# Three query groups of each batch with weights stationary in the second product of a two-batch attention block

## The reference, cut to what matters

```
qkv  = x @ w_attn + b_attn                  # x: (2, 4096, 256), float32
attn = softmax(q @ k.T / 16 + causal mask)  # per batch, 4096 x 4096
x    = layernorm(x + (attn @ v) @ w_proj + b_proj)
scores = x @ w_router;  top = the 3072 highest of 4096 per batch
x    = layernorm(x + (gelu(x @ w_block) for rows in top, x for the others))
```

## Time and profile before

| | |
|---|---|
| time, median of 3 runs | 978.8 us (977.38 to 978.82) |
| the profiled execution's own time | 978.79 us, of which the span is 977.1 us |
| TensorE (PE) busy | 942.2 us, 96% of the span, 4940 matmuls |
| weight loads (PEld) busy | 800.5 us, 82%, beside the matmuls |
| VectorE busy | 768.5 us, 79% |
| ScalarE busy | 638.7 us, 65% |
| GpSimd busy | 281.1 us, 29% |

### The profile page before, as it was taken

One profiled execution on the slowest core, in us unless ns is written; L12 is line 12 of the kernel. 1 busy time (PEld: TensorE's weight loads), 2 busy tenths in 40 slices (PEclk: granted clock), 3 DMA queues, 4 the chain that ended last, 5 costly groups with the idle time before them and its releaser, 6 DMA issues.

```text
span 977.1 us, 15396 instructions
## 1 busy us (share of the span) xinstructions
PE 942.2 (96%) x4940; PEld 800.5 (82%) x4940; DVE 768.5 (79%) x1472; ACT 638.7 (65%) x1006; POOL 281.1 (29%) x436
## 2 busy tenths in 40 slices
PE   8899999999999999999999999999999999998991
PEld 6788888888888888888888888888788888887770
DVE  5789697966876695688688979797898789549877
ACT  3466576764864595478466757567698668438893
POOL 5422214324041033514232231422403303201162
PEclk9999999999999999999999999999999999999996
DMA  6543343443343345567632433434678634427835
GB/s 203 195 136 108 98 152 119 129 136 102 108 151 109 97 130 162 159 197 239 208 120 85 159 119 98 141 108 156 200 248 280 195 97 124 143 79 251 305 102 173
DMA packets 89378, 149.52 MB, mean 153 GB/s; under 512 B 7761, under 2 KB 25810, under 8 KB 89298
## 3 DMA queue, kind: packets, MB, share of 16 engines
q1 hardware_dynamic: 89298, 148.54, 47.8%
HBM read 108.66 MB, written 39.85 MB: 152 GB/s over the span
## 4 chain that ended last, share of the span: by engine, by line
PE 87%; DVE 6%; issue 2%; ACT 2%; POOL 1%; DVEq 0%; ACTq 0%; POOLq 0%
PE sbank L507 36%; PE fbank L507 12%; PE obank L1022 11%; PE obank L1020 11%; PE obank L1021 11%; PE fbank L1101 1%; PE fbank L1294 1%; DVE ring_lo L986 1%; PE mbank L936 1%; DVE tail L1706 1%; DVE ring L967 1%; PE mbank L957 1%; DVE runmax L898 1%; ACT ring L974 1%; ACT parts L981 0%
## 5 line engine op out<-in xcount | busy, mean ns | idle before, releaser
L507 PE MATMUL sbank<-qT,xT 128*128 128x512 f32 (+2 forms) x1728 | 409.8, 377 | 1.5 <-issue 1.5
L507 PEld LDWEIGHTS sbank<-qT,xT 128*128 128x128 f32 x1728 | 305.7, 188 | 55.2 <-issue 2.2
L861 ACT COPY ring<-sbank 128x512 f32<-128x512 f32 (+3 forms) x288 | 157.4, 549 | 173.8 <-PE sbank L507 116.5
L1020 PE MATMUL obank<-ring_lo,vs 128*128 128x512 f32 (+3 forms) x576 | 218.8, 380 | 5.1 <-issue 1.7
L1022 PE MATMUL obank<-parts,vs 128*128 128x512 f32 (+3 forms) x576 | 216.1, 375 | 0.0
L1021 PE MATMUL obank<-parts,vs 128*128 128x512 f32 (+3 forms) x576 | 215.8, 375 | 0.0
L986 DVE TENSOR_TENSOR ring_lo<-ring,parts 128x1024 fp32r<-128x1024 f32 (+4 forms) x176 | 178.6, 1025 | 26.5 <-ACT parts L981 25.5
L903 DVE TENSOR_TENSOR runmax<-ring,runmax 128x1024 f32<-128x1024 f32 x84 | 106.1, 1264 | 89.0 <-ACT ring L861 88.2
L981 ACT CAST parts<-ring 128x1024 fp32r<-128x1024 f32 (+4 forms) x176 | 145.5, 834 | 46.8 <-PE obank L1022 46.5
L967 DVE TENSOR_TENSOR ring<-ring,mbank 128x1024 f32<-128x1024 f32 (+4 forms) x176 | 159.6, 949 | 8.4 <-PE mbank L957 8.4
L974 ACT ACTIVATE ring<-ring 128x1024 f32<-128x1024 f32 (+4 forms) x176 | 144.0, 845 | 16.9 <-DVE ring L967 16.7
(11 more groups left out here) (214 smaller groups left out, 1004.8 us busy)
## 6 DMA issues: line engine op xcount, KB each, us to landing
vs<-v_scratch SPq DMA_DIRECT2D x288, 256.0 KB, 2.8
v_scratch<-vnew SPq DMA_DIRECT2D x30, 512.0 KB, 3.1
xres<-x SPq DMA_DIRECT2D x16, 512.0 KB, 4.5
out<-tail SPq DMA_DIRECT2D x32, 256.0 KB, 3.3
x_scratch<-xres SPq DMA_DIRECT2D x14, 512.0 KB, 3.0
y_scratch<-yb SPq DMA_DIRECT2D x14, 512.0 KB, 4.3
tail<-x_scratch SPq DMA_DIRECT2D x28, 256.0 KB, 3.1
tail<-y_scratch SPq DMA_DIRECT2D x28, 256.0 KB, 3.9
```

The source lines that it names most:

```text
L507: mm = eng.matmul(o, lhs(lh, k), rhs(rh, k), start=n == 0, stop=n == len(todo) - 1)
L861: act.copy(slot(n)[:, c0:], sbank[n % NSS][:, c0:]).then_inc(a_copy, 1)
L1020: pe.matmul(o, vh, lo_, start=i == 0, stop=False)
```

## The change

The constant `STRAIGHT` = 3 marks the groups g = 0, 1 and 2 of each batch (G = 0, 1, 2, 8, 9, 10). For these:

- in `values` the scores become the stationary factor (128 keys by 128 queries) and the values stream (256 channels). A tile makes three matmuls of 256 columns for each block of 128 queries that it meets, into `obank[t // 2]`, so the outputs stand there with queries on the partitions. Each bank then takes two query blocks; only the first matmul into a bank has the start flag;
- there is no copy to `ot_sb`, no transpose and no `("o", G, j)` fill; `evac` reads `obank` itself once the group's last tile is done;
- the next group's first tile of `values` waits for `v_h`, that is, for the four additions of `evac`, and no longer for `a_ot`.

The counts of `a_ot` are taken over the other ten groups (`turned`). The tables of the planner, `PREFER_US` and `MARGIN_US`, get other numbers as well.

```diff
+STRAIGHT = 3
 PREFER_US = {"ffn flo": 100, "final load": 100, "project xlo": 100, "last chain": 60, "last router": 60,
-             "row_max reduce": 60, "project qhi": 60, "attention_out residual": 60, "project qlo": 60,
-             "attention_out stats": 60, "ffn fhi": 60, "scores copy": 30, "softmax hi": 30, "final scale": 30,
-             "row_max": 8, "scores hide": 8, "prepare xlo": 8, "project xhi": 8, "project vhi": 8,
-             "project vlo": 4, "softmax lo": 4, "ffn gelu": 4, "softmax exp": -4, "softmax z": -4,
-             "final result": -4, "ffn aggr": -8, "attention_out router": -8, "late": -8, "attention_out aggr": -8,
-             "final pick": -15, "attention_out score": -30}
+             "project qhi": 60, "attention_out residual": 60, "project qlo": 60, "attention_out stats": 60,
+             "ffn fhi": 60, "attention_out score": 60, "scores copy": 30, "softmax hi": 30, "final pick": 15,
+             "row_max": 8, "scores hide": 8, "prepare xlo": 8, "project vhi": 8, "row_max reduce": 4,
+             "project xhi": 4, "project vlo": 4, "softmax lo": 4, "ffn gelu": 4, "project load": 4,
+             "attention_out evac": 4, "softmax exp": -4, "softmax z": -4, "final result": -4, "ffn aggr": -8,
+             "attention_out router": -8, "late": -8, "attention_out aggr": -8, "attention_out istd": -8,
+             "final scale": -15, "final choose": -30, "prepare": -30}
...
-             "out": 1.5, "scores hide": 1, "values load": 0.6, "ffn aggr": 0.6, "final_roots": 0.6,
-             "row_max reduce": 0.3, "project load": 0.3, "proj": 0.3, "ffn stats": 0.3, "last": 0.3,
-             "attention_out stats": 0.3}
+             "out": 1.5, "scores hide": 1, "ffn store": 1, "values load": 0.6, "ffn aggr": 0.6,
+             "final_roots": 0.6, "row_max reduce": 0.6, "project load": 0.3, "proj": 0.3, "ffn stats": 0.3,
+             "last": 0.3, "attention_out stats": 0.3}
...
+    straight = lambda G: groups[G][1] < STRAIGHT
+    turned = lambda G: sum(not straight(H) for H in range(G))
...
-        out_fills += [("o", G, 0), ("o", G, 1)] + (block_fills(G) if G < LATE else [])
+        out_fills += ([] if straight(G) else [("o", G, 0), ("o", G, 1)]) + (block_fills(G) if G < LATE else [])
...
                 if i == 0:
-                    if G:
-                        pe.wait_ge(a_ot, CC * G)
+                    if G and straight(G - 1):
+                        pe.wait_ge(v_h, QT * G)
+                    elif G:
+                        pe.wait_ge(a_ot, CC * turned(G))
...
-                for c in range(CC):
+                for t in range(i or 0, QT) if straight(G) else ():
+                    o = obank[t // 2][:, t % 2 * C:(t % 2 + 1) * C]
+                    own = slice(t * P - c0, (t + 1) * P - c0)
+                    vh, vl = (vs[:, n % NV, h, :] for h in range(2))
+
+                    pe.matmul(o, lo_[:, own], vh, start=i == 0 and t % 2 == 0, stop=False)
+                    pe.matmul(o, hi_[:, own], vh, start=False, stop=False)
+                    mm = pe.matmul(o, hi_[:, own], vl, start=False, stop=t % 2 == 1 and (last or g == 0 and i == t))
+                for c in () if straight(G) else range(CC):
...
-            at("act", "attention_out ot", lambda act: ot(act, 0))
-            if G < len(groups) - 1:
+            if not straight(G):
+                at("act", "attention_out ot", lambda act: ot(act, 0))
+            if not straight(G) and G < len(groups) - 1:
                 at("act", "attention_out ot", lambda act: ot(act, 1))
...
-            o_halves = lambda j: bank_of(("o", G, j))[:, :].rearrange("p (t c) -> p t c", t=2)
+            o_bank = lambda j: obank[j] if straight(G) else bank_of(("o", G, j))
+            o_halves = lambda j: o_bank(j)[:, :].rearrange("p (t c) -> p t c", t=2)
...
             def evac(dve, j):
-                filled(dve, ("o", G, j))
+                if straight(G):
+                    dve.wait_ge(p_pv, first_tile[G + 1])
+                else:
+                    filled(dve, ("o", G, j))
...
-            for j in range(2):
+            for j in range(0 if straight(G) else 2):
                 pe_fill[("o", G, j)] = lambda pe, j=j: turn(pe, j)
```

More of the change, by code:

```diff
@@ L477, in freed @@
                 elif bank_no[f] == 5:
-                    eng.wait_ge(a_ot, CC * (len(groups) - 1) + 1)
+                    eng.wait_ge(a_ot, CC * turned(len(groups) - 1) + 1)
                 elif bank_no[f] >= 3:
@@ L1082, in last_ot @@
                 dve.tensor_copy(ot_sb[:, 1, :], obank[1][:, :]).then_inc(v_ot, 1)
-            at("act", "attention_out ot", lambda act: ot(act, 0))
-            if G < len(groups) - 1:
+            if not straight(G):
+                at("act", "attention_out ot", lambda act: ot(act, 0))
+            if not straight(G) and G < len(groups) - 1:
                 at("act", "attention_out ot", lambda act: ot(act, 1))
-            else:
+            elif not straight(G):
                 at("dve", "attention_out ot", last_ot)
-            o_halves = lambda j: bank_of(("o", G, j))[:, :].rearrange("p (t c) -> p t c", t=2)
+            o_bank = lambda j: obank[j] if straight(G) else bank_of(("o", G, j))
+            o_halves = lambda j: o_bank(j)[:, :].rearrange("p (t c) -> p t c", t=2)
             def turn(pe, j):
                 if G < len(groups) - 1:
-                    pe.wait_ge(a_ot, CC * (G + 1))
+                    pe.wait_ge(a_ot, CC * (turned(G) + 1))
                 else:
-                    pe.wait_ge(a_ot, CC * G + 1)
+                    pe.wait_ge(a_ot, CC * turned(G) + 1)
                     pe.wait_ge(v_ot, 1)
```

## The result

The changed kernel took 973.82 us, median of 4 runs (973.07 to 974.12); the kernel before, on the same chip, 978.81 (977.38 to 979.12, 4 runs). The ratio on record is 0.9945 with a 95% interval of 0.993 to 0.996 (the two medians alone give 0.9949): 5.0 us or 0.5% faster, against a prediction of 974.0. The profiled execution took 973.79 us, 971.8 of them span, where before it was 977.1.

A forecast was written before the change was run, and what follows sets the result against it. The prediction took PE (TensorE) as the limit from 52 to 885 us; −5.2 − 1.9 + 2.1 = −5.0 us, −4.8 without G = 0's tiles, so 978.8 − 4.8 = 974.0 us, with an 8-in-10 range of 969.5 to 981.0 us.

The forecast's parts named there:

- PE bound from 52 us on: From 52 to 885 us PE is busy 830.93 of 833 us, so only the number and form of its matmuls count.
- Transposes, −5.2: 48 of the 128 transposes of `ot_sb` go, each worth 0.109 us of PE: 5.2 us saved.
- Tiles of 128, −1.9, and of 512, +2.1: Second product: six 128-wide tiles save 0.31 us each; thirty 512-wide tiles, as twelve 256-column matmuls, cost 0.07 us more each.
- the sum with G = 0: PE's terms together, −5.0 us; without G = 0's own tiles, which lie where PE waits anyway, −4.8 us.
- The rule beside the sum: Trainium skill's 109 ns for 256 columns, weight loads hidden, against 0.119 us from the rows: would give 969.3 us; not followed.
- Copies, 0: 12 ACT copies to `ot_sb` go, 7.1 us of ACT, priced at nothing because PE doesn't wait for ACT.
- The wait for `evac`, 0: Next group's first tile waits for DVE's additions, 2.25 us at most: priced 0, bounds 0 and 6 × 1.2 us.
- The order, 0 ± 3: New planner tables reorder operations on all engines; free inside PE's full stretch, waits outside may close or open: 0, ±3 us.
- rivals B and C: New order closes idle places outside the full stretch, 971 us (chance 0.12), or loses 3 us, 977 to 978 (0.17).
- Rival A: The new 256-wide matmuls run at the weights' pace, 0.112 us instead of 0.119: 3.3 us less, 970.7 us; chance 0.08.

The follow-up runs named there:

- halves: Kernel before, planned order untouched, each of the 224 full second-product tiles made as twelve 256-column matmuls instead of six of 512: 995.91 us, ratio 1.0166.
- turned_thrice: Kernel before, planned order untouched, each transpose of `ot_sb` issued three times in all groups but the last (240 more): 1005.91 us, ratio 1.0266.
- evac_late: Changed kernel, planned order untouched, with a 2.3 us reduction on DVE ahead of each of the six `evac` of changed groups: 980.65 us, ratio 1.0003.
- the filled kernels: Changed kernel and kernel before, each with 25 matmuls on constants in PE's waits near start and end: 972.31 us (ratio 0.9932) and 978.85 us (0.9997).
- the other counts: Changed kernel with 1, 2, 4 or 7 straight groups a batch instead of 3: 980.37, 977.12, 982.42 and 988.64 us.
- kept_warm: Changed kernel, planned order untouched, with 14 matmuls on constants in PE's waits between 22 and 33 us: 974.24 us, ratio 0.9942.

## Why the prediction was right

*PE bound from 52 us on: right.* The same windows stand at 99.8% after, and the time follows the number of places on PE, in halves and in turned_thrice as in the change.

*Transposes, −5.2: right.* 0.109 each was the price, and an added transpose in turned_thrice takes 0.109. A fill of four takes only 0.354 us until the next start, because what follows starts 0.028 us behind the last one; but this next matmul then holds its own place for 0.315 us instead of 0.228. Together that is 0.110 for each, −5.3. (So a mean of the distances behind the transposes alone, 0.092, would be too low a price; the earlier trace rows show the same, 18 matmuls in 4.20 us instead of 4.10.)

*Tiles of 128, −1.9, and of 512, +2.1: right.* By mean distances −1.7 and +1.9 (30 × (12 × 0.1193 − 6 × 0.228)); halves gives 0.076 a tile instead of 0.07, or 0.064 without the slower scores. Over all matmuls PE's work fell by 5.1 us, against −5.0 in the sum with G = 0, of which the forecast used −4.8.

*The rule beside the sum.* The Trainium skill's section that the prediction names gives 109 ns as the gap of an isolated matmul. For a stream of pairs of weight load and matmul it gives other figures, about 81 ns at 128 columns and 131 ns at 512, and the prediction left that out. Here pairs of float32r went at 0.107 to 0.112 and 0.228 us, so none of these figures fits.

*Copies, 0: right by the windows*; ACT lost 12 of them and PE's full stretch didn't become fuller. No run takes copies away alone.

*The wait for `evac`, 0: right in the sum, wrong in its room.* I claimed 3 us at the tightest place and called G = 2 to 3 that place. The room is 1.7 us there, and 0.9 at G = 10 to 11, where the gap of PE shrank from 16.1 to 5.9 us in the new order: I had read the gaps of the old order. With 2.3 us of delay at each of the six (evac_late) the gain was gone, though direct waits were only 1.9 us of it.

*The order, 0 ± 3: right for this pair of tables, by luck in part.* Against the closed waits (−2) stands the fall of the clock (+1.6), which I hadn't in the sum at all; the filled kernels show what the change is worth without it, 6.5 us. For this pair of tables rivals B and C are worth some 2 us at most by the medians. The ground for the term was wrong: I held that inside the full stretch an order costs nothing as long as PE has work. The kernel before had waits there (0.39 and 0.84 us), and for the other counts the order was worth up to 9 us by the medians and 14 by the spans, three times my bound and more: had I been asked for those, I would have missed.

*Rival A* is refuted by the pace in the changed kernel (0.12 and not 0.112) and by halves.

## What to carry to other kernels

Where one engine is full, price a change by the distances of starts on it and not by the records' durations or by busy time: here this gave PE's work to within 0.3 us of 5. That the time came out within 0.2 us of the forecast was luck: two terms of some 2 us weren't in the sum. Where a planner writes the order, the price of the changed operations is only half of the matter: any edit gives a new order whose waits, far from the edit, can be larger than the gain, so count them from the new trace before believing a price, and measure the room at a hand-over in the new order. A wait on TensorE can cost more than its length, since the clock may fall behind it; matmuls on constants in such waits gave 2 us of span in one profiled execution of the changed kernel (1.3 by the ratios, with intervals that overlap), and nothing in the kernel before.

## What was not expected of the hardware

- The clock fell to half beside waits of 1.4 to 3.9 us in some executions and not in others, with the same wait at the same place (1.41 us at 887 to 889 us: full clock in the changed kernel, half in kept_warm). In three traces it fell at 17 us, where the last wait above 0.2 us was one of 0.72, 8 us earlier. Falls inside otherwise full work cost 1.4 to 1.7 us each for 3.4 us at half. What decides stays open.
- Matmuls of 512 columns for the scores go at 0.2282 to 0.2287 us, but at 0.2302 and 0.2303 in the two kernels with most 256-wide matmuls, though they are unchanged themselves. Why isn't shown.
- 128 columns take 0.107 to 0.112 us, 256 columns 0.1193, 512 columns 0.228 with a fresh weight each (float32r): below 256 columns a shorter stream saves almost nothing.
- What follows the last of four transposes starts 0.028 us behind it and then takes 0.315 us instead of 0.228 to the next start: the transpose's place is 0.109 to 0.110 us all the same.
